# Four small VectorE operations made into one in every split norm, and the scan's first norm moved from the last to the fourth block of a mixture of experts

## The reference, cut to what matters

```python
def _layernorm(x, axis=-1, eps=1e-05):
    m = jnp.mean(x, axis=axis, keepdims=True)
    v = jnp.var(x, axis=axis, keepdims=True)
    return (x - m) / jnp.sqrt(v + eps)

x = x + _layernorm(_step(_layernorm(x), weights...))      # eight times:
# L0 attention, L0 linear with a low-rank part, L1 windowed attention, L1 mixture of 16 experts (two of them chosen),
# L2 selective scan, L2 ternary MLP, L3 attention with position bias, L3 ternary MLP
```

## Time and profile before

| | us |
|---|---|
| median of 3 runs | 4467.24 |
| lowest, highest | 4465.38, 4478.55 |
| profiled execution | 4461.61 |
| its span on the core | 4459.5 |
| output projections `l0o`, `l1o`, `l3o` | about 841 to 891, 1212 to 1271, 4182 to 4233 |
| linear layer `l0f` | about 891 to 953 |
| collecting of results in `l1f` | about 1515 to 1619 |

### The profile page before, as it was taken

One profiled execution on the slowest core, in us unless ns is written; L12 is line 12 of the kernel. 1 busy time (PEld: TensorE's weight loads), 2 busy tenths in 40 slices (PEclk: granted clock), 3 DMA queues, 4 the chain that ended last, 5 costly groups with the idle time before them and its releaser, 6 DMA issues. The chain is left out here.

```text
span 4459.5 us, 103263 instructions
## 1 busy us (share of the span) xinstructions
PE 3974.1 (89%) x39268; PEld 2151.5 (48%) x39268; DVE 3387.1 (76%) x5859; ACT 2842.8 (64%) x4508; POOL 2061.6 (46%) x1888
## 2 busy tenths in 40 slices
PE   8899999877869942499999999999998999999888
PEld 4344444554638620245445454454454555555555
DVE  8899999565654469888888888887226888888586
ACT  3577777654444235688887888876124777777664
POOL 5122222331234549888888888878000222222322
PEclk9899999989978975699999999999998999999999
DMA  4211111014323434365555655555323222222000
GB/s 144 60 37 37 38 36 40 12 35 115 75 99 105 124 106 105 97 173 143 147 156 141 179 147 144 157 143 159 94 66 127 60 68 61 61 69 60 29 10 29
DMA packets 263623, 411.12 MB, mean 92 GB/s; under 512 B 52636, under 2 KB 139708, under 8 KB 263076
## 3 DMA queue, kind: packets, MB, share of 16 engines
q1 hardware_dynamic: 233480, 376.07, 30.6%
q0 software_dynamic: 6912, 18.88, 1.7%
q10 hardware_dynamic: 22848, 11.02, 1.0%
HBM read 351.85 MB, written 53.24 MB: 91 GB/s over the span
## 5 line engine op out<-in xcount | busy, mean ns | idle before, releaser
L1016 DVE CUSTOM_DVE_ANT_0 banks<-banks,l3s_table 128x1024 f32<-128x1024 f32 x512 | 620.1, 1240 | 100.7 <-PE banks L936 91.0
L1099 ACT ACTIVATE l3s_probs<-banks 128x512 f32<-128x512 f32 x1024 | 542.2, 595 | 230.2 <-PE banks L936 115.8
L2744 POOL TENSOR_TENSOR l_dbx<-l_u,l_bc 128x1024 f32<-128x1024 f32 x256 | 602.3, 2353 | 179.5 <-DVE l_u L3186 65.0
L1011 DVE TENSOR_REDUCE l0s_peak<-banks 128x1 f32<-128x1024 f32 x512 | 605.2, 1213 | 65.5 <-PE banks L936 64.7
L1099 ACT ACTIVATE l0s_probs<-banks 128x512 f32<-128x512 f32 x1024 | 536.1, 601 | 172.2 <-PE banks L936 170.4
L2754 POOL TENSOR_TENSOR l_ys<-l_ys,l_hc 128x1024 f32<-128x1024 f32 x232 | 547.8, 2361 | 41.8 <-DVE l_hc L3206 37.4
L3000 ACT ACTIVATE banks<-l_dt,l_decay 128x512 f32<-128x512 f32 x512 | 345.4, 686 | 218.4 <-DVE banks L3195 215.2
L2897 PE MATMUL banks<-l_ha,l_ring 128*128 128x512 f32 x1024 | 446.7, 593 | 0.1
L2897 PE MATMUL banks<-l_hb,l_ring 128*128 128x512 f32 x1024 | 442.9, 593 | 1.5 <-DMA l_ring<-in_l2f_stream 1.4
L3195 DVE TENSOR_TENSOR_SCAN banks<-banks,l_carry,l_dbx 128x512 f32<-128x512 f32 x256 | 329.5, 1289 | 76.1 <-ACT banks L3000 49.5
L3195 DVE TENSOR_TENSOR_SCAN banks<-banks,l_dbx 128x512 f32<-128x512 f32 x256 | 314.1, 1228 | 67.3 <-ACT banks L3000 39.3
(11 more groups left out here) (513 smaller groups left out, 7241.8 us busy)
## 6 DMA issues: line engine op xcount, KB each, us to landing
l_bc<-l_bc_rows SPq DMA_DIRECT2D x256, 512.0 KB, 5.3
l_ring<-in_l2f_stream SPq DMA_DIRECT2D x176, 512.0 KB, 6.5
l3s_table<-bias_table SPq DMA_DIRECT2D x16, 960.0 KB
qk_parts<-l0s_probs SPq DMA_DIRECT2D x96, 128.0 KB, 2.4
qk_parts<-l3s_probs SPq DMA_DIRECT2D x32, 384.0 KB, 3.4
y_rows<-l1f_out_b SPq DMA_DIRECT2D x80, 128.0 KB, 1.7
l0s_q_st<-qk_parts SPq DMA_DIRECT2D x64, 96.0 KB
l0s_k_st<-qk_parts SPq DMA_DIRECT2D x64, 96.0 KB
```

Of the source, the lines that this page charges most:

```text
L1011: nc.vector.tensor_reduce(out=peak[:, b % 2, t:t + 1], in_=s1[t % 2], axis=AX, op=ALU.max, negate=True).then_inc(s1_used, 1)
L1016: nc.vector.tensor_tensor_reduce(out=s1[t % 2], in0=s1[t % 2], in1=rows, scale=1.0, scalar=LOW, op0=ALU.add, op1=ALU.max, accum_out=peak[: ...
L1099: nc.scalar.activation(columns(probs[b % 2][:, t, :], half * 512, (half + 1) * 512), scores, ACT.Exp, scale=scale).then_inc(s2_used, 1)
L2744: nc.gpsimd.tensor_tensor(dbx[:, at:at + 2], u[:, 2 * mh:2 * mh + 2], bc[:, load % BR, 0].unsqueeze(1).to_broadcast([P, 2, TB]), ALU.mult)\
```

## The change

Two things are changed. `SplitNorm.vector` writes the shift with one scalar_tensor_tensor, (mean * -1.0) * r on four columns, in place of four tensor_scalar of one column; its two inputs `mean_var` and `rstd` are both tensors in SBUF. This holds for all 47 calls. And the scan's first norm is made in iteration 3 of the mixture's loop in place of iteration 7, in VectorE's part and in POOL's.

```diff
     def vector(self, v, n):
         wait(v, self.rstd_ready, n + 1)
-        for k in range(BT):
-            last = self.nc.vector.tensor_scalar(self.shift[:, k:k + 1], self.mean_var[:, k, 0:1], self.rstd[:, k:k + 1],
-                                                -1.0, ALU.mult, ALU.mult)
-        last.then_inc(self.shift_ready, 1)
+        self.nc.vector.scalar_tensor_tensor(out=self.shift[:], in0=self.mean_var[:, :, 0], scalar=-1.0, in1=self.rstd[:],
+                                            op0=ALU.mult, op1=ALU.mult).then_inc(self.shift_ready, 1)
...
             for n in range(NB):
-                if n == NB - 1:
+                if n == 3:
                     wait(v, added, 1)
                     following.statistics(v, lambda k: chip.x[:, k, :])
                 combine(n)
...
             for n in range(NB):
-                if n == NB - 1:
+                if n == 3:
                     following.gpsimd(g, 0)
                 posts[n % 2].gpsimd(g, n // 2)
```

## The result

| | before | after |
|---|---|---|
| median (runs) | 4467.69 us (6) | 4502.03 us (6) |
| lowest, highest | 4463.23, 4478.55 | 4499.02, 4504.68 |
| profiled execution, its span | 4461.61, 4459.5 | 4499.02, 4497.2 |

The changed kernel takes 1.0072 of the time, 95% interval 1.0061 to 1.0083: 34.3 us more by the medians and 37.4 by the two profiled executions. The forecast was 4498, with +28.1 us in the projections and +5.8 in the mixture, counted from a base between 4461.6 and 4467.2.

A forecast was written before the change was run, and what follows sets the result against it. POOL's additions would hold the shift, making VectorE's 5.6 us round the projections' pace; POOL's gathers pace the mixture's end. 28.1 + 5.8 = +33.9 us, giving 4495.5 (profiled base) or 4501.1 (median); forecast 4498, range 4462 to 4509.

The forecast's parts named there:

- +5.8 in the mixture: Mixture: POOL's stream 7.3 us late from block 3 after the norm's move, less 1.5 us at the end.
- The undisturbed shift: Single four-column shift operation with no POOL addition beside it: 0.20 us in place of 0.58, a gain of 0.37 each.
- The gain of 4.8 us: Projections, nothing held: 13 calls in `l0o`, `l0f`, `l1o` and `l3o` at 0.37 us each.
- The hold: Projections: the two-input shift waits for POOL's running addition to end, +1.8 us on VectorE each, 21 of 47 calls.
- POOL 0.06 ahead keeps it: Earlier trace row: POOL, 0.06 us ahead of VectorE, kept its 1.05 us; so POOL's addition was taken as first.
- Rival 1: VectorE first at the lock: nothing held, projections gain 4.8 us, mixture loses 5.8, 4462.6 us; chance 0.20.
- it did nothing until POOL was through: Row 3174, a two-input scalar_tensor_tensor started inside a POOL addition: it ended 1.08 us after POOL, 1224 ns at best.
- The stages: Projections' losses from holds: `l0o` +9.1, `l1o` +7.7, `l3o` +7.0, `l0f` +4.3, sum +28.1 us.
- VectorE's wait of 3.48 us before block 6: In `l3o`: this wait was to take 3.5 us off the 5.7 us lost up to block 5.
- line 1424 of block 6: In `l3o`: the later addition was to hold this operation, adding 1.2 us.
- The drain: Mixture's block 3: drain waits for gathers in flight, ending 7.83 us after the last gather's issue; POOL 7.3 us late.
- The end: Mixture's end: ScalarE's two last applications follow each other, ending at 1613.85 instead of 1615.32, -1.5 us.

The follow-up runs named there:

- e1 to e8: Experiments, each an edit of the kernel before, on two chips where that kernel took 4474.27 us (e1 to e4) and 4478.04 us (e5 to e8).

## Why the prediction was right, and where it wasn't

- **The undisturbed shift** takes 0.16 us, not 0.20, 0.42 less than the four. The gain of 4.8 us where nothing is held is not shown at that size. The version with waiting additions is at about -4 us by the ratio, between -8 and 0. In its profile the four stages take 217.9 us together, against 220.6 before and 219.2 to 220.5 in the six other experiments that keep the old shift: 1.2 to 2.6 less. A part may go to line 1424 (1425 there), which now meets the later additions (median 404 ns in `l0f`, in place of 170). By the Trainium skill's rule of few operations (VectorE: DVE Perf Modes, Rules for kernel authors) the change had to gain; with POOL first it lost, and with VectorE first the gain is at the edge of what can be told.
- **The hold.** 21 of 47 calls held, in the blocks named, for 2.16 to 2.32 us, each to the end of the addition. "POOL 0.06 ahead keeps it" was the right row to go by. Rival 1 (VectorE first) is what the waiting additions turned into fact, and it gave 4457.63 beside 4465.98. One reading was a little off: row 3174 has 1.08 us left after POOL's end, less than its 1224 ns at best, so "it did nothing until POOL was through" holds only to some 0.15 us.
- **The stages.** `l0o` +8.6 (9.1 expected), `l0f` +4.2 (4.3), `l1o` +6.5 (7.7), `l3o` +9.2 (7.0): 28.6 for 28.1, and +27 by the run of the shift alone. In `l1o` the shift's delay, counted from the stage's first statistics, fell from 3.8 us in block 5 to 3.1 in block 6, where VectorE waits 5.34 us for POOL in both kernels; I had taken nothing off there. The step that failed is in `l3o`. I let VectorE's wait of 3.48 us before block 6 take up 3.5 of the delay. After the change it still waits 3.38 us there (second row below), since what it waits for had become late too. And line 1424 of block 6 isn't held there (0.17 us at 4258.61), for which I had added 1.2. Without the two terms my sum is 5.7 + 3.6 = 9.3, close to the 9.2 measured. The timeline of after:

```profile
4253.11 0.16 DVE L1433 SCALAR_TENSOR_TENSOR l3o_post_shift<-l3o_post_mean_var,l3o_post_rstd 128x4 f32<-128x4 f32 x1 [1.13 <-POOL l3o_post_rstd L1428]
4256.66 1.42 DVE L1419 BATCH_NORM_STATS2 l3o_post_stats<-banks 128x6 f32<-128x256 f32 x4 [3.38 <-PE banks L397]
```

- **The drain** was mis-sized and its mechanism was wrong. I took 7.83 us from the last gather's issue to the drain's end; it was 4.87 (1592.02 to 1596.89), 1.96 less by the drain itself and 1.0 by the r that had stood in between. From the first to the seventh r the results took 5.05 us longer (68.98 and 74.03), in place of 7.3.
- **The end** of the mixture gained 1.41 us from the seventh r on (14.78 and 13.37), 1.5 expected. ScalarE's two last applications do follow each other. In sum the results cost 3.6 in place of 5.8, and the norm's move alone 4.5 by its ratio, with an interval from 0 to 9.
- **The total** of 33.9 stands against 34.3 by the medians. That it is so near is partly luck: the mixture was 2.2 too high, `l1o` 1.2 too high and `l3o` 2.2 too low, and the stretches that the change touches sum up to 32.2 in the two profiles, the rest being 5.5 us elsewhere.

## What to carry to other kernels

Before several small VectorE operations are fused into one, look at what POOL does at that moment. Here one that reads two SBUF tensors was held to the end of a POOL tensor_tensor that was ahead by some hundredths of a us, and 0.16 us turned into 2.3. If it must stand there, let POOL's long operation wait for it; here that cost nothing that could be measured, and a short filler didn't do it. A wait that a profile shows takes up a delay only if what it waits for isn't made late by the same delay.

## What the runs showed of the hardware that I had not expected

- A drain on POOL took 5.63 us with no gather in flight, and the one in the same place 2.12 or 1.06 when another drain had stood 24 or 8 gathers before it. Without a drain POOL's idle time at the end of the stage rose to 6.29 us instead, in both such versions.
- As in the earlier trace rows, POOL can be the one held: with VectorE's addition 0.11 us ahead at the end of the mixture, POOL's r took 1.98 us in place of 1.04 (1640.38 and 1640.49 above).
- With both records beginning at 866.68, it was VectorE's operation that was held.
- In eight profiles, one of them with nothing changed but the memset in the projections, the third r of the results came about 20 us after the second, in place of 11.1. VectorE waited there for gathered rows, whose gathers had all been issued some 15 us earlier, and went on 3.7 to 4.5 us after the issue of the next block's last gather. The other profiles don't have it. The eight are those of e1 to e8, from two of the three chips. The kernel before took 4474 to 4478 us beside them and 4466 to 4468 beside the rest, which would fit the same wait in it, but no profile of it was taken there, and the cause is open.
